# Cross-attention scores behind both halves of the linear quad's scores in every other round, and the maxima bounded by a tensor_scalar

## The reference, cut to what matters

```python
# D: linear attention, 16 heads of 16, 64 features, causal
qp, kp = relu(q @ proj), relu(k @ proj)
aw = (qp @ kp.T) * mask
out_D = (history + aw @ v) / (normaliser + 1e-6) @ Wout + bout
x = layernorm(x + out_D)
# E: cross-attention, 16 heads of 16, keys and values from ctx
attn = clip((q @ k.T) * 0.25, -10000, 10000)
out_E = softmax(attn) @ v @ Wo + bo
x = layernorm(x + out_E)
```

## Time and profile before

| | us |
|---|---|
| median of 3 runs | 1573.2 (1571.88 to 1577.44) |
| profiled execution | 1566.94 |
| its span, first to last instruction | 1564.9 |
| stages D and E side by side, about | 755 to 1065 |
| stage E alone | 1065 to 1200 |

### The profile page before, as it was taken

One profiled execution on the slowest core, in us unless ns is written; L12 is line 12 of the kernel. 1 busy time (PEld: TensorE's weight loads), 2 busy tenths in 40 slices (PEclk: granted clock), 3 DMA queues, 4 the chain that ended last, 5 costly groups with the idle time before them and its releaser, 6 DMA issues.

```text
span 1564.9 us, 23343 instructions
## 1 busy us (share of the span) xinstructions
PE 1326.4 (85%) x9071; PEld 1118.8 (71%) x9071; DVE 1075.8 (69%) x1729; ACT 570.1 (36%) x1171; POOL 800.9 (51%) x762
## 2 busy tenths in 40 slices
PE   6996999999989989977798989896582798989890
PEld 6985788778868868855566766665452798989890
DVE  4655766766676676543777677677673688888886
ACT  3666211211111021123344444443330565666552
POOL 4343666656656566523222433534443776767652
PEclk9997999999999999999999999998685899999995
DMA  5100333233223233212233215323400855555525
GB/s 167 37 21 1 111 94 115 81 92 98 81 81 99 76 94 94 61 39 56 94 99 120 82 40 120 88 58 95 115 8 25 293 211 192 209 191 207 192 71 161
DMA packets 58044, 163.23 MB, mean 104 GB/s; under 512 B 10598, under 2 KB 26185, under 8 KB 50000
## 3 DMA queue, kind: packets, MB, share of 16 engines
q1 hardware_dynamic: 45760, 100.13, 22.2%
q0 software_dynamic: 12176, 61.63, 11.1%
HBM read 136.47 MB, written 27.08 MB: 105 GB/s over the span
## 4 chain that ended last, share of the span: by engine, by line
PE 60%; DVE 17%; issue 7%; DMA 6%; ACT 5%; SPq 3%; POOL 2%; ACTq 0%; POOLq 0%; DVEq 0%
PE bank L388 13%; PE bank L390 13%; PE bank L389 13%; PE bank L1210 9%; PE bank L396 4%; SPq L717 3%; DVE topE L1714 2%; DVE hid_hi L1589 2%; DMA split_qk<-qk_lo 2%; PE bank L1052 2%; DVE shiftE L1723 2%; DMA xt_hi<-split_qk 2%; DVE hf L1605 2%; PE bank L1039 1%; PE bank L1128 1%
## 5 line engine op out<-in xcount | busy, mean ns | idle before, releaser
L520 POOL TENSOR_TENSOR wpiece_lo<-wraw,wpiece_hi 128x1024 fp32r<-128x1024 f32 x88 | 216.9, 2464 | 7.4
L1591 DVE TENSOR_TENSOR hid_lo<-hf,hid_hi 128x512 fp32r<-128x512 f32 x96 | 213.8, 2227 | 3.3
L388 PE MATMUL bank<-hid_hi,wpiece_lo 128*128 128x512 f32 x512 | 202.4, 395 | 12.9 <-DVE hid_lo L1591 12.9
L390 PE MATMUL bank<-hid_hi,wpiece_hi 128*128 128x512 f32 x512 | 200.7, 392 | 0.0
L389 PE MATMUL bank<-hid_lo,wpiece_hi 128*128 128x512 f32 x512 | 200.7, 392 | 0.0
L518 POOL TENSOR_SCALAR wpiece_hi<-wraw 128x1024 fp32r<-128x1024 f32 x88 | 95.0, 1080 | 186.2 <-PE bank L390 182.3
L1589 DVE CAST hid_hi<-hf 128x512 fp32r<-128x512 f32 x96 | 79.6, 830 | 125.7 <-ACT hf L1326 124.6
L1326 ACT ACTIVATE hf<-bank,ffn_scales 128x512 f32<-128x512 f32 x64 | 44.2, 690 | 293.8 <-PE bank L390 293.8
L636 POOL TENSOR_SCALAR staging<-staging 128x1024 f32<-128x1024 f32 x64 | 66.7, 1041 | 138.9 <-ACT staging L1411 138.6
L1210 PE MATMUL bank<-w_hi,gh_lo 128*128 128x256 f32 x368 | 106.1, 288 | 22.5 <-issue 21.8
L388 PEld LDWEIGHTS bank<-hid_hi,wpiece_lo 128*128 128x128 f32 x512 | 96.8, 189 | 39.1 <-DVE hid_lo L1591 19.3
(11 more groups left out here) (337 smaller groups left out, 3711.4 us busy)
## 6 DMA issues: line engine op xcount, KB each, us to landing
wraw<-in_C_w SPq DMA_DIRECT2D x88, 512.0 KB, 3.6
split_qk<-qk_hi SPq DMA_DIRECT2D x64, 128.0 KB, 2.4
split_qk<-qk_lo SPq DMA_DIRECT2D x64, 128.0 KB, 2.4
xt_lo<-split_qk SPq DMA_DIRECT2D x8, 1024.0 KB, 5.5
xt_hi<-split_qk SPq DMA_DIRECT2D x8, 1024.0 KB, 6.9
yc<-y_rows SPq DMA_DIRECT2D x16, 256.0 KB, 6.2
ctx_raw<-in_ctxT SPq DMA_DIRECT2D x16, 192.0 KB, 3.7
xraw<-in_xT SPq DMA_DIRECT2D x8, 256.0 KB, 3.5
```

The lines of the kernel that those rows point to most:

```text
L388: pe.e.matmul(o, sl, mh, start=start and i == 0, stop=False)
L390: made = pe.e.matmul(o, sh, mh, start=False, stop=stop and i == n - 1)
L520: pool.e.tensor_tensor(pair[1], raw, f(pair[0]), ALU.subtract).then_inc(done, 1)
L1591: dve.e.tensor_tensor(lo[:, o, :], hf[o % 2][:, :], f(hi[:, o, :]), ALU.subtract).then_inc(s_hid, 1)
```

## The change

In even rounds (p even) the pair's scores get priority 4.5 in place of 0. They then come behind QUAD's steps 1, 3 and 2 (priorities 2, 3 and 4) and ahead of everything with priority 5. In odd rounds they stay first. Besides, the bound on the maxima is one `tensor_scalar` with two constants instead of one `scalar_tensor_tensor` that took the lower limit from a tile; the tile `lowE` and its memset on POOL go. Line numbers behind the change are 1 to 4 lower.

```diff
@@ de_steps @@
-        items += [(e + p, (0, 1, 2), "PAIR", (b, p), (0, 2, 4)) for p in range(PAIRS)]
+        items += [(e + p, (0 if p % 2 else 4.5, 1, 2), "PAIR", (b, p), (0, 2, 4)) for p in range(PAIRS)]
@@ build @@
-        low_e = sbp("lowE", [P, 2 * TT])
@@ pool_program @@
-            pool.e.memset(low_e[:, :], -lim).then_inc(s_vone, 1)
@@ vector_program, values @@
-                dve.wait_ge(s_vone, 4)
+                dve.wait_ge(s_vone, 3)
@@ vector_program, PAIR step 0 @@
-                    dve.wait_ge(s_vone, 4)
-                    dve.mark(dve.e.scalar_tensor_tensor(out=top[:, :], in0=top[:, :], scalar=lim, in1=low_e[:, :], op0=ALU.min,
-                                                        op1=ALU.max))
+                    dve.mark(dve.e.tensor_scalar(top[:, :], top[:, :], lim, -lim, ALU.min, ALU.max))
```

## The result

| | before | changed |
|---|---|---|
| median, same chip | 1575.9 us (12 runs) | 1586.6 us (12 runs) |
| ratio to before | | 1.0069 (95%: 1.0043 to 1.0096) |
| profiled execution | 1566.94 us | 1576.03 us, the fastest of its 12 |

The change is slower by 0.7%, about 11 us, where 28 us of gain were forecast. In the changed kernel L1050 is the quad's scores, L1105 the pair's, L1063 aw @ v, L1126 the values' product, L1037 the feature matmul, L395 a transpose; on DVE L1712, L1714 and L1719 are maximum, bound and shift, L1694 the mask product. The experiments have the same numbers unless said otherwise.

What follows compares the result with a forecast made beforehand. PE was taken as the bound, 89% busy where stages D and E overlap. 25.7 + 2.3 + 2 + 7, less 2.2 and 7, gave 28 us: 1545 from the median 1573.2; low end 1532, high end 1566.

Steps and rivals of the forecast that it cites:

- Steps 1 to 4: Double banks of both halves, even pair and odd pair: waits of 2.3 and 25.7 us gone, both pairs covered at cost 0.
- step 1: First half needs the odd pair's shift; 1.02 us of transposes ahead of it cover waits of at most 0.63; 2.3 gone.
- The 25.7 and 2.3 us: PE's waits for DVE's shift before the quad's and the pair's scores, both forecast to go entirely.
- The term of 2 us for the transposes: Transposes now stand ahead of the wait in the chain of keys and queries: 2 us gained, bounds 0 and 4.
- the 2.2 us not harvested: Two average waits of 1.12 us whose saving turns into longer waits in the chain of keys and queries.
- What is late next: Small DVE work behind the even pair delays the odd pair's shift: 7 us of new waits, bounds 0 and 14.
- Step 5: Feature matmul needs the even pair's shift: 3.75 us of DVE covered by 3.92 of PE work; 0 for most rounds.
- The clock: Low granted clock in three stretches, with PE no longer idle ahead of them: 7 us regained, bounds 0 and 8.3.
- The bound: New form of DVE's bound on the maxima, which may be held up like the old: 0, bounds -5 and +2.
- Slower: Rival: feature matmul in the odd round waits for the even pair's shift, up to 2.65 us a quad; 1594 us, chance 0.08.
- Only half: Rival: DVE's small work makes the odd pair's shift late in most rounds, 14 us of new waits; 1559 us, chance 0.15.
- The queries' chain: Rival: savings in rounds within it return as waits at the next sequence's first pair, 12 us; 1557 us, chance 0.12.

Runs made afterwards that it cites:

- the best version: Changed kernel with the even pair's scores right behind the quad's first half, sequence 0's first two even pairs in the old place; ratios 0.9862 and 0.9843 to before.
- order-only kernel: Kernel before with the new order alone, the bound keeping its old form and its tile lowE; ratio 1.0043 to before.
- the tile kept: Changed kernel with the tile lowE still allocated, written and read by nothing; ratio 1.0061 to before.
- first half, first rounds spared: Changed kernel, even pair's scores right behind the quad's first half, except sequence 0's first two even pairs, in the old place; ratios 0.9862 and 0.9843 to before.
- first rounds spared in the changed kernel: Changed kernel, but sequence 0's first two even pairs keep the old place ahead of the transposes; one run, no ratio, quads' stretch 378.2 us.

## Why the prediction was wrong

**What held.** Steps 1 to 4 as to the double banks, nearly: no second half waits for the shift, four first halves do (4.2 us, 1.4 at most, so the 1.02 of cover in step 1 is too little there), and the odd pair's scores wait 0.7 us in three for the mask. Three of the four (1.19, 1.41 and 1.40 us) stand behind a bound that stood still; without any bound the four are 0.8 us together. The 25.7 and 2.3 us went. The term of 2 us for the transposes and the 2.2 us not harvested are settled by no run. The bound's form is worth nothing, as said.

**The step that failed** is "What is late next". It said that the small DVE work, now 2.65 us lower, "then delays the odd pair, whose shift the next first half needs", and priced it at 7 us with 14 as a bound. It looked only at the double banks. The small work also drains the single banks, which PE needs for the values' product and the transposes one round on. PE waited 23.7 us for those and 8.9 for the double banks, 32.6 in place of 7. With that, and with no clock back, the prediction's own sum gives 25.7 + 2.3 + 2 - 2.2 - 32.6, or 4.8 us slower, beside the 4.3 us by which the stretch grew. The experiment that reordered DVE alone shows it: with the small work in its old position no wait for a single bank is left.

**Step 5** was covered in the round that was worked through, which the prediction called the shortest. It is not: in the first rounds of stage E's first sequence there is no values' product (1.00) and at first no transposes (1.02) behind the odd pair. There the feature matmul waits 2.08 and 1.78 us, nearly all of its 4.0, and the changed kernel lost 5.9 us between quads 9 and 12, the slow clock behind the first wait included; sparing those rounds gave 5.4 back there.

**The clock** gave back nothing of the 7 us. The same work keeps PE busy for 324.5 us before and 324.9 after; it would have needed the waits to go, and they only moved. Where they did go, in the best version, busy time fell by 11.3 us. In the 31 runs of before on one chip the mean granted clock was 0.925, in those of the order-only kernel 0.922 and with the tile kept 0.921, and among the runs of before each 0.01 goes with 12 us. By this estimate some 4 to 6 us of the loss can be the clock's. With the 4.3 of the stretch that would match the 7 to 11 us of the medians, but the two may overlap, since the mean clock takes in the stretch, and that a lower clock and a longer run go together does not say which brings which. Where the rest of the 7 to 11 us lies is argued, not shown.

**The bound** was put at 0 with -5 and +2. In the old place that was right. In the new order it meets POOL's low parts and x_tok additions: its stalls over 0.4 us up to 1080 add up to 12.6 us in place of 7.5 (the 0.17 of the instruction itself taken off), and three of them stand right ahead of the 2.09 us waits. I had read the stalls of the earlier trace rows as DVE time and not asked what their place beside POOL would become.

**The rivals.** "Slower" had the right sign for another place: the feature matmul cost 4 us, not 51. "Only half" had named DVE's small work behind the even pair, but for the odd pair's shift, at 14 us of new waits; the first halves' waits for that shift were 4.2. The queries' chain did not decide here, but it is what comes next: of the 14.0 us of the earlier trace rows 5.5 are left in the changed kernel, and 10.8 to 19.8 us stand in the kernels whose waits for DVE are under 19 us.

## What to carry to other kernels

When work on an engine is moved behind something long, list every buffer ring that the work then queued behind it drains, not only the ring that the move is about. A wait that goes because a consumer comes later is worth nothing if the engine it waited for has the same work in a thicker heap: here it paid to put the pair between the two halves, where DVE had otherwise been idle. And a round that is worked through must include the first ones of the pipeline, in which part of the cover does not exist yet.

## What was unexpected in the hardware

- A DVE tensor_scalar of 128x4 with SBUF operands only took 0.17 us, and up to 2.41 beside POOL. All of the 12 stalls over 0.4 us in the changed kernel up to 1080 end 0.02 to 0.04 us behind the end of a POOL instruction, and a stall can last through several: at 884.27 it outlasted the low part and both x_tok additions, at 778.07 (0.89 us) the low part and only the first of the two. What decides this stays open. The old form, on the tile, was held in the same way (13 times, up to 1.26 us).
- tensor_reduce on SBUF operands of like size was never held, 128 times out of 128 (160 to 165 ns). The Trainium skill ("SBUF — State Buffer", Who interferes with whom) says that tensor_reduce never contends on this chip, and these rows agree.
- The same matmuls of the quads' stretch kept PE busy for 313 us at a granted clock of 0.97 (first half, first rounds spared) and for 329 us at 0.92 (first rounds spared in the changed kernel).
